# A Mamba block's product with the spread B, taken over two PSUM banks at a time and placed between two scans

## What is computed

```python
w  = dt * u                                   # 128 channels
dA = exp(dt[:, :, None] * A)                  # 128 channels x 16 states
h  = dA * h + w[:, :, None] * B[:, None, :]   # the recurrence over the tokens
y  = einsum('bdn,bn->bd', h, C) + u * D
y  = y * silu(z)
out = einsum('bld,ed->ble', y, out_proj_w)
```

## Time and profile before

| | |
|---|---|
| median of 3 runs | 2034.57 us |
| the profiled execution's own time | 2032.55 us |
| its span, first to last instruction | 2030.8 us |
| VectorE busy, share of the span | 1483.5 us, 73% |
| TensorE matmul busy | 1643.1 us, 81% |
| GpSimd busy | 1216.9 us, 60% |
| ScalarE busy | 981.5 us, 48% |
| mean granted TensorE clock | 0.952 |
| the two Mamba blocks' products with B | 45.1 to 1663.9 us, 768 of them |

### The profile page before, as it was taken

One profiled execution on the slowest core, in us unless ns is written; L12 is line 12 of the kernel. 1 busy time (PEld: TensorE's weight loads), 2 busy tenths in 40 slices (PEclk: granted clock), 3 DMA queues, 4 the chain that ended last, 5 costly groups with the idle time before them and its releaser, 6 DMA issues. The chain is left out here.

```text
span 2030.8 us, 31247 instructions
## 1 busy us (share of the span) xinstructions
PE 1643.1 (81%) x7952; PEld 1124.3 (55%) x7953; DVE 1483.5 (73%) x2441; ACT 981.5 (48%) x1739; POOL 1216.9 (60%) x1409
## 2 busy tenths in 40 slices
PE   6888888888878399999946888888888874699994
PEld 4444444444435299999934444444444433599992
DVE  4999999999995522222246999999999986444443
ACT  6777677766763011111137777667766643011111
POOL 1888888888882135454305888888888860355440
PEclk8999999999999699999977999999999997799996
DMA  4344433333336301011033334433333326011114
GB/s 157 128 141 142 143 134 125 125 125 125 125 125 259 135 32 38 34 39 34 29 118 125 126 134 141 144 143 126 125 125 125 125 82 276 27 52 46 46 44 148
DMA packets 60049, 227.06 MB, mean 112 GB/s; under 512 B 8448, under 2 KB 23680, under 8 KB 56576
## 3 DMA queue, kind: packets, MB, share of 16 engines
q1 hardware_dynamic: 51744, 203.93, 28.1%
q0 software_dynamic: 8256, 22.56, 3.4%
HBM read 206.92 MB, written 19.53 MB: 112 GB/s over the span
## 5 line engine op out<-in xcount | busy, mean ns | idle before, releaser
L657 POOL TENSOR_TENSOR L_hc<-L_h,L_crep 128x384 f32<-128x384 f32 x768 | 775.2, 1018 | 211.1 <-DVE L_h L586 211.1
L382 PE MATMUL ps<-L_hc,ident 128*128 128x384 f32 x1536 | 622.4, 487 | 0.9 <-POOL L_hc L657 0.8
L577 DVE TENSOR_TENSOR ps<-L_w,ps 128x384 f32<-128x384 f32 x768 | 414.9, 540 | 20.4 <-PE ps L373 10.4
L487 ACT ACTIVATE L_da<-L_dt,L_negA 128x384 f32<-128x384 f32 x768 | 414.9, 604 | 15.6 <-DVE L_h L586 15.0
L373 PE MATMUL ps<-L_parts,sel 96*128 96x384 bf16 x768 | 256.3, 335 | 183.6 <-DVE L_h L586 177.3
L586 DVE TENSOR_TENSOR_SCAN L_h<-L_da,L_carry,ps 128x384 f32<-128x384 f32 x384 | 384.6, 1002 | 0.0
L586 DVE TENSOR_TENSOR_SCAN L_h<-L_da,L_h,ps 128x384 f32<-128x384 f32 x384 | 383.6, 999 | 0.0
L373 PEld LDWEIGHTS ps<-L_parts,sel 96*128 96x128 bf16 x768 | 73.4, 96 | 501.7 <-DVE L_h L586 494.3
L382 PEld LDWEIGHTS ps<-L_hc,ident 128*128 128x128 f32 x1536 | 270.9, 193 | 39.4 <-issue 6.2
L1114 DVE COPY Xn<-L_w 128x2048 f32 x86 | 107.8, 1256 | 117.6 <-PE ps L1064 108.8
L1097 ACT ACTIVATE L0e_hT<-ps 128x512 f32<-128x512 f32 x86 | 51.4, 597 | 267.4 <-PE ps L1064 267.4
(11 more groups left out here) (270 smaller groups left out, 2052.0 us busy)
## 6 DMA issues: line engine op xcount, KB each, us to landing
L_crep<-c_rows SPq DMA_DIRECT2D x192, 768.0 KB, 7.6
L_w<-in_up SPq DMA_DIRECT2D x16, 1024.0 KB, 11.9
L_w<-in_down SPq DMA_DIRECT2D x8, 1024.0 KB, 26.9
tok_rows<-Xn SPq DMA_DIRECT2D x6, 768.0 KB, 13.1
L0s_got<-results SPq DMA_DIRECT2D x18, 256.0 KB, 2.8
L1s_got<-results SPq DMA_DIRECT2D x18, 256.0 KB, 3.3
L_w<-in_down SPq DMA_DIRECT2D x8, 512.0 KB, 21.3
X<-in_x SPq DMA_DIRECT2D x4, 576.0 KB, 7.7
```

Of the source, the lines that this page charges most:

```text
L382: nc.tensor.matmul(y_ps[r], ident[:], hc[:, n % NHC, :], start=False, stop=(n == N - 1)).then_inc(sem["y"], 1)
L487: nc.scalar.activation(da[:, n % NDA, :], dt[:, r, :], ACT.Exp, scale=negA[:, 0, n:n + 1]).then_inc(sem["da"], 1)
L577: nc.vector.tensor_tensor(b_ps(n), w[:, r, :], b_ps(n), ALU.mult).then_inc(sem["dbu"], 1)
L657: nc.gpsimd.tensor_tensor(hc[:, n % NHC, :], h[:, n, :], crep[:, r, n, :], ALU.mult).then_inc(sem["hc"], 1)
```

## The change

`times_b` takes a pair j of states instead of one. The two banks of a pair lie side by side (0 and 1, or 3 and 4), and one VectorE instruction multiplies both by `w`, which is repeated for the second bank. There are 8 of them per tile instead of 16. It waits until both banks' spreads are there. The product of pair j + 1 is issued after the scan of the even state n = 2j, so it stands between the scans of n and n + 1, which read the other bank pair; before, a product stood ahead of every scan. The first product of the next tile stands after the scan of n = 14. The counts that `scan` and GpSimd wait for on the semaphore `dbu` are halved to match. TensorE's order, its LEAD and the banks stay as they were.

```diff
+        def b_two(j):
+            at = (0, 3)[j % 2]
+            return ps[:, at:at + 2, 0:T]
...
-            def times_b(t, r, n):
-                g = t * N + n
-                dve.wait_ge(sem["b"], g + 1)
-                if n == 0:
+            def times_b(t, r, j):
+                g = t * N + 2 * j
+                dve.wait_ge(sem["b"], g + 2)
+                if j == 0:
                     dve.wait_ge(sem["w"], t + 1)
-                nc.vector.tensor_tensor(b_ps(n), w[:, r, :], b_ps(n), ALU.mult).then_inc(sem["dbu"], 1)
+                two = b_two(j)
+                nc.vector.tensor_tensor(two, w[:, r, :].unsqueeze(1).to_broadcast([P, 2, T]), two, ALU.mult
+                                        ).then_inc(sem["dbu"], 1)
 
             def scan(t, n, slot):
                 g = t * N + n
                 dve.wait_ge(sem["da"], g + 1)
-                dve.wait_ge(sem["dbu"], g + 1)
+                dve.wait_ge(sem["dbu"], t * (N // 2) + n // 2 + 1)
...
             def tile(t, r, p, slot, last):
                 for n in range(N):
-                    if n + 1 < N:
-                        times_b(t, r, n + 1)
-                    elif not last:
-                        times_b(t + 1, 1 - r, 0)
                     scan(t, n, slot)
+                    if n % 2 == 0:
+                        if n + 2 < N:
+                            times_b(t, r, n // 2 + 1)
+                        elif not last:
+                            times_b(t + 1, 1 - r, 0)
...
-                            wait(pool, sem["dbu"], t * N)
+                            wait(pool, sem["dbu"], t * (N // 2))
```

## The result

The changed kernel took 2045.02 us (median of 5 runs, 2044.43 to 2047.75), the kernel before 2032.19 us (median of 5 runs, 2031.06 to 2036.46). The ratio is 1.0062, with a 95% interval of 1.0047 to 1.0077: slower by 0.6%, 12.8 us between the medians.

The account below looks back on a forecast made before the run. VectorE was taken to bound the Mamba blocks (busy 98.89 of 100 us). Terms -19.2 - 1 - 1 + 8.8 + 16.1 + 2.8 = +6.5 us on a median of 2034.57 gave 2041.1 us, range 2026 to 2055.

Parts of the forecast that it names:

- The instructions: VectorE's 768 products become 384 of twice the length, each followed after 0.85 us where two took 0.90: -19.2 us.
- the turns: Loop turn after the carry copy: the product there was already hidden, so less is saved: +8.8 us at 22 turns.
- the start: Start of each block: both first products are made while VectorE waits for the token's state: -1 us.
- The stall at the residual: Step 8: pair 6's product waits for the spread of 13, queued behind z_in; 0.54 us even, 0.22 odd tiles: +16.1.
- The first tiles: First tile of each block, slow clock: pair 4's product waits 1.4 us for its bank: +2.8 us.
- Extras: Residual, gate, splits on VectorE: the product behind one paid 0.46 us instead of 0.45, about 180 places: -1 us.
- Scans back to back: Two scans in a row on VectorE: the second starts 0.90 to 0.92 us after the first, priced at nothing.
- The product behind an extra: VectorE product after residual, gate or splits: 0.46 us instead of 0.45, about 180 places, 1 us gained.
- Scans: Scans now in a row on VectorE: distance of 0.90 to 0.92 us taken as unchanged, priced at nothing.
- the second stall at ScalarE: Rival: silu_z and a table load delay the decay of n = 12; 13 us on top, 2054; chance 0.14.
- The instruction does what it says: Answers the rival that crossing banks or repeating w costs 0.90 or more, losing the 19.2: 2060; chance 0.08.
- The product in time for the gain: Rival: spread of 13 ready by R + 2.09 (R: residual's start), no stalls: -12.4 us, 2022; chance 0.12, 0.05 for half.

Follow-up runs that it names:

- e9: Changed kernel with residual after n = 7, split_two after n = 5, and pair 1's product before scan n = 0 in even tiles but the first: 2011.99 us.
- e1: Changed kernel with one constant changed, the residual after the scan of n = 7 instead of n = 8: 2027.27 us, ratio 0.9978 to the kernel before.
- e2: Changed kernel with split_two moved from after n = 4 to directly after the scan of n = 5, ahead of the gate: 2037.5 us, ratio 1.0026.
- e3: Changed kernel with the merge undone in place, two products of 384 elements where one of 768 stood: 2052.08 us, ratio 1.0097.
- e8: Changed kernel with residual after n = 7, split_two after n = 5, and the merge undone in place: 2038.42 us, ratio 1.0032.
- e5: Changed kernel with the next even tile's first product issued after the carry copy and loop turn: 2051.12 us, ratio 1.0102.
- e7: Changed kernel with residual after n = 7, split_two after n = 5, and even tiles' first product behind the loop turn: 2032.94 us, ratio 1.0003.
- e11: Changed kernel with residual after n = 7, split_two after n = 5, and each merged product right in front of its own scan: 2092.96 us, one time only.

## Why the prediction was right, and where it was not

The forecast was slower, 2041.1, with 2026 to 2055; measured were 2045.0, and 12.8 us more than before instead of 6.5. The absolute number looks better than it is, for the forecast stood on a median of 2034.57 for the kernel before; on the 2032.19 measured with the change it would be 2038.7. The direction and what decides it were right; the difference was twice the one forecast. Term by term, from the distances between VectorE's starts in the two traces:

- *The instructions, the turns, the start.* Forecast -19.2, +8.8 and -1, in all -11.4. From the first scan to the last one of each block, the distances behind products fell from 347.5 to 325.4 us, and those behind the `carry` copy rose from 14.2 to 23.4: -12.9. With -0.9 for the start, which lies ahead of the first scan, it is -13.8. The 0.85 was exact, and so was the thought that the product at the turn had been hidden; e9 shows it by hiding another.
- *The stall at the residual.* Forecast 0.54 and 0.22 us, 16.1 in all. Measured 0.51 and 0.23, 15.9 in all, and e1 took 17.8 us away. Right in place, size and cause.
- *The first tiles.* Forecast 2.8; the two products are 1.33 and 1.80 us late, 3.1.
- *Extras.* Forecast 1 us gained from what follows them. The products behind an extra had cost 0.015 us more at 184 places, 2.8 us, which are gone and stand in the first term. The scan behind the residual and `split_one` pays 0.02 too: 1.4 us lost. Net 1.4 gained.
- *`split_two`.* The step that was wrong. "Scans back to back ... The product behind an extra" priced the extras by what VectorE does behind them, and looked at GpSimd only as one that waits. That `split_two` reads two SBUF tensors, and whether GpSimd would be at work when it is issued in the new rhythm, was not asked. It cost 46 x 0.20 = 9.4 us; e2 got 7.5 of it back.
- *Scans.* Priced at nothing; they brought 4.1 us. The second of two scans in a row is mostly followed after 0.905 us, not 0.92, here and in every variant in which scans stand in pairs, e3 and e8 with their single products too.

Without the start these make -12.9 + 15.9 + 3.1 + 1.4 + 9.4 - 4.1 = 12.8 us, what was measured in the blocks. Two terms without a price in the prediction, 9.4 and -4.1, partly cancel. That the result still lies within the forecast's 2038 to 2048 is in part luck. A tile takes 23.95 us (odd) and 24.88 (even), 24.4 on the mean, where 24.2 to 24.3 was forecast.

Of the rivals, the second stall at ScalarE did not come in the changed kernel; it stood just behind, with 20 waits of 0.2 us when e3 shortened the first stall. The instruction does what it says. The product in time for the gain came only with e1.

## What to carry to other kernels

When two waits are merged into one, the merged one needs the later of its inputs at the time of the earlier: look in the producer's own order for what stands ahead of that input, not at its idle share. Here one constant in the consumer's order (the residual two instructions earlier) turned a loss of 0.6% into a gain, and three such moves gave 2012.0 us, 1.0% below the kernel before. On an engine that is full, an instruction less is worth its share of the distance between starts (0.054 us here), not the fixed part of its duration; and a change of rhythm can cost a neighbour that was not touched.

## What was not expected of the hardware

- A VectorE instruction with two SBUF inputs and GpSimd's products hold each other up in either order: 0.20 us on VectorE, or 0.29 on GpSimd, by who starts first. A copy of 16 columns from SBUF to SBUF is held as well, to 0.03 us behind the end of GpSimd's product (66 times in e5, e7 and e11), and six times through a second one, up to 1.52 us. The `gate` and `split_one`, with one input in SBUF and one in PSUM, are not (0.54 us for 0.52, 0.60 for 0.58).
- A scan that reads what the instruction right before it wrote, and waits for it, starts 1.02 to 1.17 us after a product of 768 elements instead of 0.85 (e11); 1.32 at a loop's turn (e5, e7).
- Behind the loop's turn VectorE needs 1.14 us from the copy to a scan, and a product that this scan does not read costs only 0.43 us more in there (0.69 + 0.88 against 1.14), not its 0.85.
- The second of two scans in a row is followed after 0.905 us, a scan behind a product after 0.92. Why was not tried.
